# Sixteen-head attentions: two sets of turned places, strips five pairs ahead, scores at the end of the step, values pair by pair

## The reference, cut to what matters

```python
# layer 0, kind "rel"
q = (w @ Wq.T).reshape(B, Lq, H, d_head).transpose(0, 2, 1, 3)   # k and v likewise
rp = (r @ Wr.T).reshape(2 * Lq - 1, H, d_head).transpose(1, 0, 2)
AC = jnp.einsum('bhid,bhjd->bhij', q + u_bias[None, :, None, :], k)
BD = jnp.einsum('bhid,hjd->bhij', q + v_bias[None, :, None, :], rp)
BD = _rel_shift(BD)
attn = jax.nn.softmax((AC + BD) * scale, axis=-1)
out = jnp.einsum('bhij,bhjd->bhid', attn, v)

# layer 1, kind "rope"
Q, K = (apply_rope(Q), apply_rope(K))
scores = jnp.einsum('bhqd,bhkd->bhqk', Q, K) / jnp.sqrt(jnp.float32(d_k))
scores = jnp.where(causal, scores, -jnp.inf)
attn = jax.nn.softmax(scores, axis=-1)
out = jnp.einsum('bhqk,bhkd->bhqd', attn, V)
```

## Time and profile before

| | |
|---|---|
| median of the runs | 6770.65 us (3 runs, 6769.74 to 6771.25) |
| the profiled execution | 6752.55 us, span 6750.8 us |
| PE, DVE, ACT, POOL busy | 5149.7, 4387.9, 3232.2, 2033.9 us |
| granted TensorE clock, mean | 0.878 |
| DMA queue of SP | 207.73 MB, 9.8% of 16 engines' span |
| `rel` attention, first to last copy of strips | 664.6 to 1365.7 us |
| `rope` attention, first to last copy of strips | 3051.3 to 3520.8 us |

### The profile page before, as it was taken

How to read it: one execution, slowest core, us unless ns; L and a number is a source line. 1 busy time by engine, 2 the same in 40 slices (tenths; PEclk the granted TensorE clock), 3 DMA queues, 4 the chain that set the end, 5 groups by cost and what they waited for, 6 DMA issues and landing times. The chain is left out here.

```text
span 6750.8 us, 113228 instructions
## 1 busy us (share of the span) xinstructions
PE 5149.7 (76%) x33132; PEld 3573.2 (53%) x33132; DVE 4387.9 (65%) x10941; ACT 3232.2 (48%) x5879; POOL 2033.9 (30%) x1374
## 2 busy tenths in 40 slices
PE   6776677667769969967777988984849657497777
PEld 5664444446657737724545755753534435343564
DVE  6995666669977737735665756755936359363774
ACT  6775766757765535535664544543030330303223
POOL 6995111149964414402213413410030000300110
PEclk8998999989989989989998999995569755698889
DMA  1000777710000000000000000000020000200000
GB/s 28 0 0 16 246 232 233 238 51 0 0 10 1 0 14 0 0 9 1 1 1 11 0 3 11 0 3 14 0 51 0 1 14 0 51 0 13 0 0 16
DMA packets 162591, 213.91 MB, mean 32 GB/s; under 512 B 54804, under 2 KB 90984, under 8 KB 162408
## 3 DMA queue, kind: packets, MB, share of 16 engines
q1 hardware_dynamic: 160360, 207.73, 9.8%
q0 software_dynamic: 2048, 4.20, 0.3%
HBM read 104.91 MB, written 106.95 MB: 31 GB/s over the span
## 5 line engine op out<-in xcount | busy, mean ns | idle before, releaser
L1795 POOL TENSOR_TENSOR l0b_S<-l0b_sim 128x1024 f32<-128x1024 f32 x256 | 494.1, 1970 | 153.4 <-ACT l0b_sim L1858 133.6
L1795 POOL TENSOR_TENSOR l0a_S<-l0a_sim 128x1024 f32<-128x1024 f32 x256 | 494.4, 1970 | 84.9 <-ACT l0a_sim L1858 62.8
L1928 DVE SCALAR_TENSOR_TENSOR l0b_w<-l0b_S,l0b_best,l0b_SG 128x1024 f32<-128x1024 f32 x256 | 311.1, 1276 | 8.7 <-ACT l0b_SG L1875 4.1
L1830 PE MATMUL l0a_WT<-ident,l0a_w 128*128 128x128 f32 x2048 | 266.2, 285 | 65.8 <-DVE l0a_w L1928 60.6
L1928 DVE SCALAR_TENSOR_TENSOR l0a_w<-l0a_S,l0a_best,l0a_SG 128x1024 f32<-128x1024 f32 x256 | 311.1, 1276 | 7.7 <-ACT l0a_SG L1875 4.1
L1830 PE MATMUL l0b_WT<-ident,l0b_w 128*128 128x128 f32 x2048 | 263.9, 282 | 65.3 <-DVE l0b_w L1928 60.0
L1830 PEld LDWEIGHTS l0a_WT<-ident,l0a_w 128*128 128x128 f32 x2048 | 235.9, 146 | 111.0 <-DVE l0a_w L1928 111.0
L830 DVE CUSTOM_DVE_ANT_0 l0att_S<-l0att_SC,l0att_BD 128x256 f32<-128x256 f32 x512 | 195.5, 419 | 151.4 <-PE l0att_SC L636 130.0
L781 ACT ACTIVATE l1att_E<-l1att_S,l1att_least 128x128 f32<-128x128 f32 (+1 forms) x512 | 215.1, 454 | 160.4 <-DVE l1att_least L830 160.4
L1830 PEld LDWEIGHTS l0b_WT<-ident,l0b_w 128*128 128x128 f32 x2048 | 232.4, 145 | 111.5 <-DVE l0b_w L1928 111.5
L1875 ACT ACTIVATE l0a_SG<-l0a_S 128x1024 f32<-128x1024 f32 x256 | 260.1, 1024 | 55.1 <-DVE l0a_w L1928 50.2
(11 more groups left out here) (707 smaller groups left out, 14456.8 us busy)
## 6 DMA issues: line engine op xcount, KB each, us to landing
shifted_rows<-l0att_XS SPq DMA_DIRECT2D x256, 384.0 KB, 2.6
l0att_BD<-shifted_rows SPq DMA_DIRECT2D x256, 256.0 KB, 2.9
enter_raw<-L_attn_w SPq DMA_DIRECT2D x4, 512.0 KB, 7.0
token_rows<-l2ar_rows SPq DMA_DIRECT2D x32, 64.0 KB, 1.5
l2ae_wgt<-L_ffn_gate_w SPq DMA_DIRECT2D x32, 64.0 KB
l2ae_wut<-L_ffn_up_w SPq DMA_DIRECT2D x32, 64.0 KB
l2ae_wdt<-L_ffn_down_w SPq DMA_DIRECT2D x32, 64.0 KB
token_rows<-l2br_rows SPq DMA_DIRECT2D x32, 64.0 KB, 1.5
```

Source lines behind the costliest of these rows:

```text
L1795: pool.tensor_tensor(S[:, h, :].rearrange("p (a c) -> p a c", a=NK), a, c, ALU.add).then_inc(sm["summed"], 1)
L1830: o = pe.matmul(WT[:, n // 4, (n % 4) * P:(n % 4 + 1) * P], w[:, h % W_RING, n * P:(n + 1) * P], ident[:, :], start=h == 0 and n % 4 == 0, ...
L1928: dve.scalar_tensor_tensor(w[:, h % W_RING, :], S[:, h, :], best[:, s, h, 7:8], SG[:, h % SG_RING, :], ALU.is_ge, ALU.mult).then_inc(sm["w ...
```

## The change

Three things are changed in both kinds. ET gets a second set of places (`[P, 2, 4, ...]`), and `values` makes one pair per step, in every step, with its two heads at two of the four column places of OT (`64 * (j % 2) + 32 * h`). The strips are made five pairs ahead instead of four. `scores` of pair j+1 moves toward the end of PE's step, behind both turns. In `rope`, SC shrinks to one set, TU gets two (NT = 2), PE's step is both turns, values, scores, `spread_out`; DVE does both shifts at the start of the step; ACT copies OT at the start of its step.

```diff
--- before.py
+++ after.py
@@ -416,14 +416,13 @@
 
 
 
-
     rel = kind == "rel"
     NH, HD, G, WIN = 16, 8, 8, 384
     NW = 3 if rel else 2
     BF = mybir.dt.bfloat16
     scale = HD ** -0.5
     BEGIN, TAIL, PAIRS = G - 1, G - 1, NB * G
-    NS = 1 if rel else 2
+    NT = 1 if rel else 2
     blocks = [(0, 0), (1, 0), (0, 1), (1, 1)] if rel else [(0, 0), (1, 0), (1, 1)]
     keys = (lambda t: L) if rel else (lambda t: P * (t + 1))
     with Phase(nc, tag) as ph:
@@ -435,12 +434,12 @@
         strips = ph.sb("strips", [P, G, NW, L + 2], BF)
         S, E = ph.sb("S", [P, 2, 2, 2, L]), ph.sb("E", [P, 2, 2, 2, L])
         least = ph.sb("least", [P, 2, 2, 2])
-        ET = ph.sb("ET", [P, 4, len(blocks), P])
+        ET = ph.sb("ET", [P, 2, 4, len(blocks), P])
         V = ph.sb("V", [P, 2, 2, NH, 32])
         OTs = ph.sb("OTs", [P, 4, L])
         rec, O = ph.sb("rec", [P, 2, NH]), ph.sb("O", [P, 2, NH, HD])
-        SC = ph.ps("SC", [P, NS, 2, 2, L])
-        TU = ph.ps("TU", [P, 4, P])
+        SC = ph.ps("SC", [P, 2, 2, L])
+        TU = ph.ps("TU", [P, NT, 4, P])
         OT = ph.ps("OT", [P, 2, L])
         PJ, EX = ph.ps("PJ", [P, 512]), ph.ps("EX", [P, 512])
         if rel:
@@ -629,11 +628,11 @@
                         return
                     p, g = 16 * b + j, j % G
                     until(pe, sm["strips_qk"], p + 1)
-                    until(pe, sm["shifted"], 4 * (p + 1 - NS))
+                    until(pe, sm["shifted"], 4 * p)
                     for t in range(2):
                         for h in range(2):
                             rows = slice(64 * h, 64 * h + 64)
-                            o = pe.matmul(SC[:, j % NS, h, t, 0:keys(t)], strips[rows, g, 0, t * P:(t + 1) * P],
+                            o = pe.matmul(SC[:, h, t, 0:keys(t)], strips[rows, g, 0, t * P:(t + 1) * P],
                                           strips[rows, g, 1, 0:keys(t)], start=True, stop=True)
                     o.then_inc(sm["scored"], 1)
 
@@ -642,9 +641,9 @@
                         return
                     p = 16 * b + j
                     until(pe, sm["exped"], 4 * p + 2 * h + 2)
-                    until(pe, sm["et_copied"], 2 * p + h)
+                    until(pe, sm["et_copied"], 2 * p + h + 1 - NT)
                     for i, (t, c) in enumerate(blocks):
-                        o = pe.transpose(TU[:, i, :], E[:, j % 2, h, t, c * P:(c + 1) * P], ident[:, :])
+                        o = pe.transpose(TU[:, h % NT, i, :], E[:, j % 2, h, t, c * P:(c + 1) * P], ident[:, :])
                     o.then_inc(sm["turned"], 1)
 
                 def spread_out(b, j, which):
@@ -671,17 +670,17 @@
                     if not exists(b, j):
                         return
                     g, n = j % G, 2 * b + j // G
-                    if g in (1, 5):
+                    if g in (0, 4):
                         until(pe, sm["ot_kept"], 2 * n + g // 4)
-                    if g == 1:
+                    if g == 0:
                         until(pe, sm["v_copied"], n + 1)
                     until(pe, sm["et_copied"], 2 * (16 * b + j) + 2)
                     for c in range(2):
                         first = 0 if rel or c == 0 else P
-                        for h in range(4):
-                            i = blocks.index((first // P, c))
-                            o = pe.matmul(OT[32 * h:32 * h + 32, g // 2 % 2, first:L], V[:, j // G % 2, c, 2 * g - 2 + h, :],
-                                          ET[:, h, i:i + 2 - first // P, :], start=c == 0, stop=c == 1)
+                        for h in range(2):
+                            i, at = blocks.index((first // P, c)), 64 * (j % 2) + 32 * h
+                            o = pe.matmul(OT[at:at + 32, g // 2 % 2, first:L], V[:, j // G % 2, c, 2 * g + h, :],
+                                          ET[:, j // 2 % 2, 2 * (j % 2) + h, i:i + 2 - first // P, :], start=c == 0, stop=c == 1)
                     o.then_inc(sm["valued"], 1)
 
                 def turn_back(n, t):
@@ -730,19 +729,26 @@
                         until(pe, sm["added"], n + 1)
                         make_values(n + 1)
 
-                def step(b, j):
+                def rel_step(b, j):
                     distance_rows(b, j + 3, 0)
-                    scores(b, j + NS - 1)
-                    spread_out(b, j + 4, "qk")
+                    spread_out(b, j + 5, "qk")
                     turn(b, j - 1, 0)
                     distance_rows(b, j + 3, 1)
-                    if j % 2 == 1:
-                        values(b, j - 2)
+                    values(b, j - 2)
                     turn(b, j - 1, 1)
-                    spread_out(b, j + 4, "v")
+                    scores(b, j + 1)
+                    spread_out(b, j + 5, "v")
                     extras(b, j)
 
-                steps(pe, step)
+                def rope_step(b, j):
+                    turn(b, j - 1, 0)
+                    turn(b, j - 1, 1)
+                    values(b, j - 2)
+                    scores(b, j + 1)
+                    spread_out(b, j + 5, "qk")
+                    extras(b, j)
+
+                steps(pe, rel_step if rel else rope_step)
 
             @block.scalar
             def _(act):
@@ -761,7 +767,7 @@
 
                 def keep_out(b, n, half):
                     if inside(b, n):
-                        until(act, sm["valued"], 4 * n + 2 * half + 2)
+                        until(act, sm["valued"], 8 * n + 4 * half + 4)
                         until(act, sm["backed"], 2 * n)
                         act.activation(OTs[:, 2 * half:2 * half + 2, :], OT[:, :, :], ACT.Copy).then_inc(sm["ot_kept"], 1)
 
@@ -783,18 +789,18 @@
 
                 def step(b, j):
                     g, n = j % G, 2 * b + j // G
+                    if not rel and g in (2, 6):
+                        keep_out(b, n - (g == 2), int(g == 2))
                     keep_rows(b, j + 3, 0)
                     raise_up(b, j, 0)
-                    keep_strips(b, j + 4)
+                    keep_strips(b, j + 5)
                     keep_rows(b, j + 3, 1)
-                    if not rel and g in (2, 6):
-                        keep_out(b, n - (g == 2), int(g == 2))
                     if not rel and g == 5 and inside(b, n - 1):
                         until(act, sm["o_turned"], n)
                         act.activation(oT[:, :], EX[:, 0:L], ACT.Copy).then_inc(sm["o_copied"], 1)
                     if g == 7 and inside(b, n + 1):
                         until(act, sm["v_made"], n + 2)
-                        until(act, sm["valued"], 4 * n + 2)
+                        until(act, sm["valued"], 8 * n + 4)
                         act.activation(V[:, (j // G + 1) % 2, :, :, 0:HD],
                                        EX[:, 0:L].rearrange("p (c h d) -> p c h d", c=2, h=NH), ACT.Copy).then_inc(sm["v_copied"], 1)
                     raise_up(b, j, 1)
@@ -827,15 +833,15 @@
                             dve.wait_ge(landed[j % 4][t], 16 * (4 * b + j // 4 + 1))
                         add = BD[:, j % 4, t, :, h] if rel else mask[:, t, 0:keys(t)]
                         dve.sem_inc(sm["passed"], 1)
-                        dve.tensor_tensor_reduce(S[:, j % 2, h, t, 0:keys(t)], SC[:, j % NS, h, t, 0:keys(t)], add, -scale, 3e38,
+                        dve.tensor_tensor_reduce(S[:, j % 2, h, t, 0:keys(t)], SC[:, h, t, 0:keys(t)], add, -scale, 3e38,
                                                  ALU.add, ALU.min, least[:, j % 2, h, t:t + 1]).then_inc(sm["shifted"], 1)
 
                 def keep_turned(b, j, h):
                     if exists(b, j):
                         p = 16 * b + j
                         until(dve, sm["turned"], 2 * p + h + 1)
-                        until(dve, sm["valued"], 8 * b + j // 2)
-                        dve.tensor_copy(ET[:, 2 * (j % 2) + h, :, :], TU[:, 0:len(blocks), :]).then_inc(sm["et_copied"], 1)
+                        until(dve, sm["valued"], 16 * b + j - 3)
+                        dve.tensor_copy(ET[:, j // 2 % 2, 2 * (j % 2) + h, :, :], TU[:, h % NT, 0:len(blocks), :]).then_inc(sm["et_copied"], 1)
 
                 def keep_strips(b, j):
                     if rel and exists(b, j):
@@ -844,7 +850,7 @@
 
                 def keep_out(b, n, half):
                     if inside(b, n):
-                        until(dve, sm["valued"], 4 * n + 2 * half + 2)
+                        until(dve, sm["valued"], 8 * n + 4 * half + 4)
                         until(dve, sm["backed"], 2 * n)
                         dve.tensor_copy(OTs[:, 2 * half:2 * half + 2, :], OT[:, :, :]).then_inc(sm["ot_kept"], 1)
 
@@ -878,6 +884,8 @@
                 def step(b, j):
                     g, n = j % G, 2 * b + j // G
                     shift(b, j, 0)
+                    if not rel:
+                        shift(b, j, 1)
                     if g in (2, 6) and rel:
                         keep_out(b, n - (g == 2), int(g == 2))
```

(5 more changed lines are left out.)

## The result

| | before | after |
|---|---|---|
| median of the runs | 6770.95 us (6769.74 to 6778.92, 4 runs) | 6698.36 us (6685.33 to 6702.12, 4 runs) |
| ratio, 95% interval | | 0.9887 (0.987 to 0.9904) |
| profiled execution's span | 6750.8 us | 6700.3 us |
| `rel`, first to last copy of strips | 701.1 us | 617.3 us |
| `rope`, first to last copy of strips | 469.5 us | 488.6 us |

The changed kernel is 72.6 us faster by the medians, where 43 had been forecast. The two stages went as forecast, one each way: `rel` lost 83.8 us (79 forecast), `rope` gained 19.1 (36 forecast). Together that is 64.7. The profiles differ by only 50.5, mostly because the stretch between the two attentions, whose code is the same in both, happened to be 13.4 us longer in this execution.

What follows compares the result with a forecast made beforehand. The prediction took both attention stages to be bound by waits in a ring of engines, no engine full. `rel` -79 and `rope` +36 gave -43, from the median 6770.65 to 6727.6 us; range 6655 to 6775.

Steps and rivals of the forecast that it cites:

- The ring of `rel`: In `rel`, the chain of waits from cast to cast: 4.43 us a step, block 38.3 against 43.24, -79 us.
- eight terms: `rel`, cast to cast: L659 0.55, turn 0.67, distance rows 0.53, values 0.27, second turn 0.96, scores 0.60, L665 0.32, cast 0.53.
- the work once per sequence: In `rel`, projections, normalizing and turning back, added to each block of eight steps: about 2.9 us kept.
- The price of the values: Values with eight records at two column places, every step: 1.07 us per pair, bounds 0.53 and 1.07.
- Rival A: Values cost half, by matmul count, in both stages: -127-13 = -140, time 6631 us; chance 0.07.
- The 1.7 us: Argument against half-price values: today's 1.07 would have to be 1.7 for sixteen records two at a time.
- The ring of `rope`: In `rope`, ACT's second exponential queues behind the strips copy, which waits for PE's last matmul: 3.8 us a step, +38 us.
- Rival B: In `rope`, ACT's ring isn't the last wait, for instance because ACT runs ahead: gain 40, time 6652 us; chance 0.12.
- The extras: In `rope`, ACT's oT and V copies add 0.7 per block, wo and projections about 0.6: 1.3 us a block.
- C: In `rel`, the transfers become the bound, deciding from 5.1 us a step: slower, 6789 us; chance 0.11.
- the floor: In `rel`, DMA moving 1.31 MB a step gives a floor of 4.0 to 4.2 us per step.
- D: The change hardly moves `rel`, every step now having values; 0.5 gained a block, `rope` unchanged: 6763 us; chance 0.08.

Runs made afterwards that it cites:

- half of the writes: The changed kernel, but inside the loop only 64 of 128 partitions of the distance rows are written to memory; 6684.2 us (1 run).
- the kernel with one head: The changed kernel, but inside the loop the values of the second head of each pair are left out; 6709.1 us (1 run).
- the repaired order: The changed kernel, but PE's `rope` step begins with the spreading of q and k, strips four pairs ahead, not five; 6604.0 us, ratio 0.9754.
- the kernel with early scores: The changed kernel, but in `rel` the scores of pair j stand behind the first distance rows, before spreading q and k; 6703.1 us, ratio 0.9899.

## Why the prediction was right

**The ring of `rel`.** Forecast 4.43, measured 4.39, and each of its eight terms within 0.07: the largest difference is the first, 0.48 for 0.55. The blocks are 37.22 for 38.3, mostly because the work once per sequence came to 2.1, not 2.9; which part of it hides wasn't followed. So a regular block gained 6.0 or more, not 4.9. The steps behind the loop's jump I had left as they were, and a jump block is still about 4 us longer (41.5 against 37.2): these five blocks gained 4.7 on average, and the three full blocks ahead of them 2.8. That 84 us came where 79 had been forecast is thus in part luck, two misses that nearly cancel. The first three full blocks, of 41.0, 38.7 and 44.3 us, are slower than later ones, and with half of the writes they are 39.1, 37.2 and 41.5; the early transfers cost a few us there that I hadn't counted.

**The price of the values.** I took 1.07 per pair between bounds of 0.53 and 1.07, for the reason that each place has four records in turn. 1.06 was measured, and the kernel with one head shows the reason: half of the records again, same 1.05. The rule in the Trainium skill (TensorEngine Tiling (Array Packing), Performance Considerations), by which operands of 32 columns allow fourfold tiling, holds: sixteen records at four places take the 0.86 that eight at two take. Rival A falls. The 1.7 us that the prediction held against it follows from no row: sixteen records of 379 ns two at a time would be 3.0.

**The ring of `rope`.** Forecast 3.8, measured 3.73; the repaired order shows that it was this ring. Rival B falls too: the strips copy waited for the spreading in practically every step, so ACT didn't run ahead. What I mis-sized is the rest of the stage, +36 forecast and +19 measured. The extras are 1.4 for 1.3, and the block 31.2 for 31.7, which makes 8 us over the stage. The larger part is the surplus of the loop's jump, which the sum left as it was: before, the six blocks with a jump were 1.6 to 3.4 us longer than the regular 29.33, 14.8 in all; in the changed kernel they are 31.2 to 31.3 like the others, 0.5 in all. Together this is some 6 us more than is missing; the first two blocks and the last steps cost that much more than forecast. The kernel before has this wait from 3080 to 3500 us, once per jump:

```profile
DVE l1att_S L830 <- issue: 15.6, 6, 2.7
```

"issue" means that nothing in the profile shows what DVE waited for. In the changed kernel DVE is idle for 2.2 us once per trip of the loop too (ahead of 3143.1, 3205.5 and 3268.0, for instance), and yet the block is only 0.1 us longer: the stall falls into the slack that the ring leaves to DVE. Where the ring is open, the jump costs again: DVE waits on "issue" 14.0 us, seven times, and jump blocks are 1.4 to 1.7 us longer than 24.19.

**The total.** -84 and +19 instead of -79 and +36 give -65 from the stages; the medians say -73, against the -43 forecast. The mechanisms were right and the size was off, above all in `rope`. The remaining 8 us lie in code that is the same, and are less than it varies by.

**The other rivals.** C, that the transfers become the bound, was wrong for this kernel, but nearer than its 0.11 sounded: plain steps shorter by 0.16 us bring it about. I had put the floor at 4.0 to 4.2 us a step, from the warm-up and from the share. The kernel with early scores waits for transfers in most blocks of 38 to 40 us, 4.7 to 5.0 a step, though the changed kernel makes the same transfers in 4.65 without waiting. So a floor worked out from a mean rate doesn't tell when transfers begin to hold a step up. D falls: `rel` did move, by 84 us.

## What to carry to other kernels

Write each engine's queue as a list, and look for a ring that closes in one step: if a copy waits for the last work of another engine's step, everything behind that copy in its queue comes late to the next step. That order, with the fifth pair that it allowed, cost `rope` 102 us and was visible before any run. Two cures of one wait don't add up: test each alone, and prefer the one that moves nothing (the second set of ET alone gave more than the whole change). And matmuls at column places cost what the longest chain at one place costs (1.05, 1.06 and 1.07 us for four records at each of one, two and four places), so filling two of four places costs the same time as filling four. A stage bound by one ring can also hide other costs, such as that of the loop's jump here, which come back when the ring is opened.

## What the runs showed of the hardware that I had not expected

Stages whose code is untouched vary by as much as many of the effects sought. Over thirteen profiles of kernels with the same code between the two attentions, this stretch took 1684.7 to 1699.0 us, and the part after `rope` 3224.2 to 3240.8. A comparison of whole times below 15 us needs many runs here, while a stage's regular block repeats to a few hundredths (37.20 to 37.25 us over the kernels with the `rel` code of the changed kernel or with one head's values).

How long a transfer takes to land isn't told by the mean rate: median landings of the writes went from 2.9 us at 269 GB/s to 4.2 us at 266, with shorter plain steps and longer waits, while in a regular block of the changed kernel they stay near 3 us at 283. Halving what is written brought them to 2.7 us.
